# Keys and values of the last pair made inside its recurrence; early routing cut into five pieces

## The reference, cut to what matters

```
x = x + linear_attention_and_ffn(_ln(x), 4 layers)
x = x + cosine_similarity(_ln(x) @ Wv.T, ctx @ Wt.T)
x = x + two_expert_gate(_ln(x))
x = x + state_space_block(_ln(x))
x = x + cross_attention(_ln(x), ctx)
x = x + top2_of_8_experts(_ln(x))

# the state space block, with 512 channels of 16 states each
h[t] = decay[t] * h[t-1] + u[t];  y[t] = sum_n h[t, n] * C[t, n]

# the cross attention, 8 heads of 64
q = x @ Wq;  k = context @ Wk;  v = context @ Wv
out = softmax(q k^T / 8) v;  return out @ Wo + bo

# the routing of 2048 rows to experts that hold 512 rows each
logits = x @ Wr + br;  topv, topi = top_k(logits, 2)
rank = cumsum(one_hot(topi).sum(1)) - ...      # place of the row at its expert
keep = rank < 512
```

## Time and profile before

| | before |
|---|---|
| time, median of 3 runs | 2595.84 us |
| lowest and highest | 2592.74 and 2601.61 us |
| profiled execution, its own time | 2597.52 us |
| its span, first to last instruction | 2595.7 us |
| PE, DVE, ACT, POOL busy, share of the span | 83%, 63%, 40%, 11% |
| granted TensorE clock, mean | 0.90 |
| last recurrence | about 1969 to 2128 us |
| its end, tail and queries | 2128 to 2180 us |
| lone cross attention | 2180 to 2284 us |
| last routing, scatter and the first fetch | 2284 to 2321 us |
| experts | 2321 to 2596 us |

### The profile page before, as it was taken

How to read it: one execution, slowest core, us unless ns; L and a number is a source line. 1 busy time by engine, 2 the same in 40 slices (tenths; PEclk the granted TensorE clock), 3 DMA queues, 4 the chain that set the end, 5 groups by cost and what they waited for, 6 DMA issues and landing times. The chain is left out here.

```text
span 2595.7 us, 31259 instructions
## 1 busy us (share of the span) xinstructions
PE 2153.1 (83%) x11024; PEld 1316.8 (51%) x11024; DVE 1633.6 (63%) x2717; ACT 1029.7 (40%) x1611; POOL 292.2 (11%) x332
## 2 busy tenths in 40 slices
PE   6999999999999988766467887888788778849994
PEld 4666666665666656533123354434354444636662
DVE  6555555555555566545999998989999983220002
ACT  1222222222222222113775876577658752212221
POOL 1111111111111111100000000010000001310005
PEclk8999999999999999877788988988899987759997
DMA  6000100000000000010110111011101102103333
GB/s 221 1 0 17 42 8 0 17 32 17 0 17 25 23 1 0 1 41 18 55 49 23 49 40 51 21 34 39 49 17 55 49 17 73 42 19 102 101 101 113
DMA packets 57469, 102.55 MB, mean 40 GB/s; under 512 B 7828, under 2 KB 39087, under 8 KB 56832
## 3 DMA queue, kind: packets, MB, share of 16 engines
q1 hardware_dynamic: 54272, 93.67, 10.9%
q0 software_dynamic: 3072, 7.28, 0.9%
HBM read 87.10 MB, written 14.94 MB: 39 GB/s over the span
## 5 line engine op out<-in xcount | busy, mean ns | idle before, releaser
L1822 PE MATMUL pa<-arena 128*128 128x512 f32 x512 | 311.3, 739 | 97.7 <-DVE arena L1392 97.6
L1384 DVE TENSOR_TENSOR_SCAN arena<-arena 128x1024 f32<-128x1024 f32 x128 | 292.4, 2284 | 7.9 <-ACT arena L831 7.5
L1608 PE MATMUL po<-arena 128*128 128x256 f32 x1024 | 230.1, 381 | 0.0
L1598 PE MATMUL pa<-arena 128*128 128x512 f32 x512 | 228.0, 598 | 0.8 <-ACT arena L679 0.8
L1822 PEld LDWEIGHTS pa<-arena 128*128 128x128 f32 x512 | 104.5, 223 | 233.8 <-DVE arena L1392 130.4
L694 ACT COPY arena<-po 128x512 f32<-128x512 f32 x64 | 37.5, 586 | 463.1 <-PE po L1563 463.1
L1608 PEld LDWEIGHTS po<-arena 128*128 128x128 f32 x1024 | 191.2, 189 | 31.8 <-issue 3.5
L544 POOL TENSOR_SCALAR arena<-arena 128x2 f32<-128x2 f32 (+1 forms) x92 | 27.6, 300 | 1557.1 <-DVE arena L1251 886.5
L815 ACT ACTIVATE arena<-arena 128x510 f32<-128x510 f32 x256 | 170.4, 716 | 60.1 <-DVE arena L1384 52.8
L1529 PE MATMUL pt<-arena 128*128 128x128 f32 x724 | 113.3, 286 | 74.6 <-DMA arena<-rows_to_experts 19.9
L1081 DVE TENSOR_TENSOR arena<-pa,arena 128x512 f32<-128x512 f32 x256 | 158.4, 681 | 26.1 <-PE pa L1543 25.3
(11 more groups left out here) (264 smaller groups left out, 3736.3 us busy)
## 6 DMA issues: line engine op xcount, KB each, us to landing
arena<-bc_rows SPq DMA_DIRECT2D x64, 512.0 KB, 4.2
arena<-in_L_ffn_W SPq DMA_DIRECT2D x16, 1024.0 KB, 7.5
arena<-in_L_attn_W SPq DMA_DIRECT2D x8, 1024.0 KB, 5.3
rows_to_experts<-arena SPq DMA_DIRECT2D x4, 1024.0 KB, 12.7
arena<-rows_to_experts SPq DMA_DIRECT2D x8, 512.0 KB, 8.6
rows_from_experts<-arena SPq DMA_DIRECT2D x8, 512.0 KB, 3.3
arena<-in_x SPq DMA_DIRECT2D x4, 512.0 KB, 7.2
arena<-in_rows SPq DMA_DIRECT2D x8, 256.0 KB, 3.2
```

The lines of the kernel that those rows point to most:

```text
L1384: v.tensor_tensor_scan(h.rearrange(flat), decay.rearrange(flat), h.rearrange(flat), 0.0, ALU.mult, ALU.add).then_inc(scan_done, 1)
L1598: last = mm(pa[(i + 2) % 4][:, :], w1[:, k, ts(i, P)], yT[:, k, :], start=k == 0, stop=k == KC - 1)
L1608: last = mm(po[s][:, ts(i, D)], gT[:, c, ts(2 * s + i, P)], w2[:, c, :], start=c == 0, stop=c == FM - 1)
L1822: last = mm(pa[c][:, :], ident, uh[i % len(uh)][:, n, :], start=g == 0 and n == 0, stop=g == NS // NG - 1 and n == NG - 1)
```

## The change

Three things are changed.

First, the keys (four steps) and the values (four steps) of the last pair are made by PE in slots 13, 15, 17, 21, 23, 25, 29 and 31 of the last recurrence (`LAST_SLOTS`), each at the end of its slot, all in the one bank `pt[0]`. ACT copies the first seven at the end of the slot behind, the eighth after the last slots of the loop. They are stored in memory whose weights are not used any more (`last_kT`, `last_vv`), since the keys and values of the pair before are still in use. PE waits for the eighth copy before the output product, which writes `pt[0]`. The four key steps in front of the tail are gone, and so are the four value steps at the start of the lone cross attention.

Second, S(0) of the lone cross attention is issued behind the queries, in front of the transposes for the router.

Third, DVE's early routing comes in pieces: `compared`, now only its first three operations, behind M(0); the rest of it, `counted`, behind M(1); `chosen` behind M(2); `ranked` behind M(3); `placed` behind M(4) and the division of tile 0; `weighed` behind M(5). The two counting products on PE go from slot 0 to slot 6. POOL's transfers for tile i wait for W(i+4) instead of W(i).

```diff
+LAST_SLOTS = (13, 15, 17, 21, 23, 25, 29, 31)
@@ POOL, send_rows
-                    pool.wait_ge(av2_done, 16 * (PAIRS - 1) + i + 1)
+                    pool.wait_ge(av2_done, 16 * (PAIRS - 1) + i + 5)
@@ ACT, mixer
+            def last_out(k):
+
+                if k < QC:
+                    late(k, last_kT[:, k, :], bank_head)
+                else:
+                    act.wait_ge(v2_done, TT * p + k - QC + 1)
+                    nc.scalar.copy(last_vv[:, k - QC, :], bank_head[:, :]).then_inc(v2_out, 1)
...
                     if q is not None:
                         cross(i)
+                    if n is None and i - 1 in LAST_SLOTS:
+                        last_out(LAST_SLOTS.index(i - 1))
...
             if p is not None:
-                for k in range(4):
+                if n is None:
+                    last_out(len(LAST_SLOTS) - 1)
+                for k in range(4) if n is not None else ():
                     late(routed + k, kT[:, k, :], late_banks[k])
@@ DVE, early_routing
                 compared(0, NT - TT)
+            if i == 2:
+                counted(0, NT - TT)
+            if i == 4:
                 chosen(0, NT - TT)
-            if i == 1:
+            if i == 6:
                 ranked(0, NT - TT, 1)
+            if i == 8:
                 placed(0, NT - TT)
-            if i == 9:
+            if i == 10:
                 weighed(0, NT - TT, 1)
@@ PE, mixer
+            def last_step(k):
+
+                bank = bank_head[:, :]
+                if k == 0:
+                    pe.wait_ge(w_cross_in, CROSS_W_IN)
+                    pe.wait_ge(ctx_in, 32 * p + 32)
+                elif k <= QC:
+                    pe.wait_ge(late_out, late_base + k)
+                else:
+                    pe.wait_ge(v2_out, TT * p + k - QC)
+                if k < QC:
+                    keys(k, bank)
+                else:
+                    values(k - QC, bank)
...
                 if n is not None:
                     head(i)
+                elif p is not None and i in LAST_SLOTS:
+                    last_step(LAST_SLOTS.index(i))
...
+                else:
+                    pe.wait_ge(v2_out, TT * p + TT)
                 for s in range(2):
...
                     queries(m)
+                if n is None:
+                    pe.wait_ge(late_out, late_base + LATE - 2)
+                    scores2(0, lone_score, last_kT)
             if n is None:
                 rows_routed()
```

More of the change, by code:

```diff
@@ L851, in cross @@
                     last.then_inc(pexp_ready, 1)
-                if i in (0, 2) and at.lone:
-                    for m in range(i, i + 2):
-                        value_out(m, lone_values)
                 if i in VALUE_COPIES and not at.lone:
-                    value_out(VALUE_COPIES.index(i), value_banks)
+                    value_out(VALUE_COPIES.index(i))
                 if i % 2 == 1 and 0 <= (i - 3 - drain) // 2 < 16:
@@ L1155, in compared, with counted @@
             step.after(v.tensor_tensor(tie, tie, mask, ALU.mult))
+        def counted(first, end):
+            up, tie = above[:, first:end], level[:, first:end]
             step.after(v.tensor_tensor(up, up, tie, ALU.add))
@@ L1823, in state_sum, with scores2 @@
                 last.then_inc(ysum_done, 1)
-            def scores2(u):
+            def scores2(u, banks=at.score, keys=last_kT if at.lone else kT):
                 tile, j, e = u // 4, u % 4 // 2, u % 2
@@ L1897, in queries @@
                 last.then_inc(late_done, 1)
+            def last_step(k):
[11 more added lines that the diff above has]
+                    values(k - QC, bank)
             def cross_scores(i):
-                if at.lone and i == 0:
-                    scores2(0)
-                    for m in range(TT):
-                        values(m)
+                if at.lone and i == 6:
                     ranks(0, NT - TT, 1)
```

47 lines of the change are left out of this document (25 added, 22 removed).

## The result

| | before | after |
|---|---|---|
| median of the runs, us | 2604.26 (13 runs) | 2587.0 (13 runs) |
| lowest and highest, us | 2589.48, 2610.44 | 2583.47, 2591.02 |
| ratio after / before, 95% interval | | 0.9949 [0.9933, 0.9966] |
| the profiled execution, us (span) | 2597.52 (2595.7) | 2588.83 (2587.0) |
| granted clock over the span | 0.900 | 0.901 |

The change is 0.51% faster: 13.3 us of 2604, with 8.9 to 17.4 us as the interval. (The ratio takes all runs into account; the two medians alone are 17.3 us apart, since the runs of the kernel before spread over 21 us.) The terms of the forecast add up to 14.2 us less (21.2 - 7.0). Its 2582 us starts from a median of three runs, 2595.84; over 13 runs that median is 2604.26. So the gain is the better comparison: 0.54% was forecast.

A forecast was written before the change was run, and what follows sets the result against it. DVE was taken to bound the last recurrence, PE the window beginning with the keys. From 2597.52 us, minus 21.2 plus 7.0 gave 2583.3; less 1.7 for a median, 2582 us, 0.54% faster, range 2572 to 2594.

The forecast's parts named there:

- Bias to W(0): Start of the lone cross attention: chain M(0), three `compared` operations, M(1), E(1), C(0) takes 6.3 us, 11.2 us less.
- the values alone: Start of the lone cross attention: values on PE are hidden beside the routing, so taking only them away gives nothing.
- W(0) to W(4): Lone cross attention: counting products add 1.2 us, `placed` instead of `weighed` saves 0.4, so 0.8 us more.
- The tail: Behind the recurrence: without the keys, transposes start 11.9 us earlier; S(0) costs 1.1, so the router's bias comes 10.8 us earlier.
- the late output product: End of the recurrence: steps in slots 29 and 31 cost about 2.0 us together, 0.8 given back for clock, 1.2 net.
- The recurrence: Last recurrence: ACT waiting for steps before copying makes scans late; costs 4.8 + 1.0 + 1.2 = 7.0 us.
- the late E in front of L1365: Last recurrence: late E before each L1365 holds up the product with Wo, 0.5 us twice, 1.0 us.
- W(4) to the end of the lone cross attention: Rest of the lone cross attention: order as before, so no change in time, 0 us.
- Full clock in the lone cross attention: Rival, lone cross attention: half clock doesn't come, turns about 3.7 us instead of 4.76, 6 us less, 2576; chance 0.18.
- The copies were not free: Rival, last recurrence: copies fit ACT's 1.81 us gap and its lead, recurrence costs 1 to 2 us, 2577; chance 0.12.
- None of the eight steps ran at half clock: Rival, last recurrence: five of seven steps meet the half clock, 11 us more, 2593; chance 0.14.
- that last rival: Slower, last recurrence: PE becomes the bound, 8 us lost per pair of units, 2598 to 2600 and more; chance 0.06.

The follow-up runs named there:

- the pieces alone: Only the early routing cut into pieces, with counting products in slot 6 and POOL's new pacing, against the kernel before: 2597.5 us, ratio 0.9991.
- the late copies: Changed kernel, but ACT copies each step two slots behind it instead of one: 2578.27 us, ratio 0.9921 to the kernel before.
- the doubled steps: Changed kernel with the first six steps done twice: 2597.09 us, ratio 0.9981; the same with copies one slot later: 2584.67 us, ratio 0.9945.
- the kernel with two a turn: Kernel with copies one slot later plus two unread 384-column matmuls per even slot from 12 on in the lone cross attention: 2571.69 us, ratio 0.9896.
- the wait in the tail filled: Five unread 512-column matmuls before the tail's transposes, added to the kernel with two unread 384-column matmuls per even slot: 2567.28 us, ratio 0.9886.

## Why the prediction was right, and where its steps were not

**Bias to W(0) (-11.5, predicted -11.2).** Right, and by the chain given: M(0), three operations of `compared`, M(1), E(1), C(0). That the values alone would give nothing was nearly right (1.7 us). What the prediction didn't say is that the pieces alone would give only 5.3. Its term for this stage was right; that the gain would last to the end was not shown by it, and is the subject of the last item below.

**W(0) to W(4) (+0.4, predicted +0.8).** Right. The turn with the counting products has 5.55 us instead of 4.76, and the division's turn 7.47 instead of 7.90.

**The tail (-11.7, predicted -9.6 with the late output product).** The wait taken away is 12.0 us by the rows, not 11.9. The start of the product was right: 1.85 us later, predicted 2.0. The clock was undersold. That product gave back 1.6 us in its first half, where I had allowed 0.8, and the queries another 1.2, where I had none: they began at half clock and did not stay there.

**The recurrence (+10.6, predicted +5.8 up to scan 31).** The mechanism was right, as the late copies and the doubled steps show, and the late scans nearly so: for a group of three 0.1, 1.6 and 0.8 us were predicted, for the units 15, 17 and 19; measured were 1.12, 0.40 and 0.80 for 17, 19 and 20, then 1.11, 0.79 and 1.52 for 25, 27 and 28, 5.7 for 4.8 in all. The waits at the units 20 and 28 were not foretold. The term that was too small is the one for the late E in front of L1365, "I take 0.5 us twice": the two waits grew from 0.74 to 2.10 and 3.69, 4.3 us more in place of 1.0. I had the E late by what its own copy costs. In the trace C(8), the tile's copy and the decays behind it all come first on ACT, so the delays add up; the second of the two also met T and the product with Wo at half clock (3.07 us for 1.90).

**W(4) to the end of the lone cross attention (+8.8, predicted 0).** "The order is as before" was true and not enough. The prediction took the clock of this stretch as unchanged, and no row said that it would be. In the ten profiles without added matmuls there, the stretch takes 64 to 74 us with nearly the same work, and its clock goes up and down: in the kernel after it is 0.65, 0.78 and 0.50 in the three windows of 4 us from 2212 on. The runs say that not all of this loss is there in every pair of runs: the four stages that the change was meant for sum up to -12.2 us, and the runs gave -13.3 [-17.4, -8.9]. With the full +8.8 it would be -3.4, which the interval excludes. The profile of before lay 6.7 us under the median of these runs, so its 64.27 us may be the better of its cases; the kernel before has one profile here, so how often it takes which case stays open, and so does what share of the +8.8 the new places of the pieces cause.

**The rivals.** Full clock in the lone cross attention did not come (0.50 in the window behind the bias). The prediction tied the fall to the wait for C(0), which shrank from 4.60 us to 0.86; the clock fell all the same, and earlier, at the end of the router's matmuls: 1.00 in the window up to 2173.8 and 0.50 from 2174 on, 6 us ahead of W(0). The copies were not free. None of the eight steps ran at half clock, each took 2.1 us; some of the T beside them and one product with Wo did. PE did not become the bound: it is busy 118.90 of 155 us. Two things in that last rival are wrong as written. Its 2598 to 2600 us are the price of three lost pairs of units; four would give about 2607. And it was not state sums that brought the clock back each time: behind scan 13 of the recurrence before, two of the five times it came back within a product with Wo.

So the forecast came true in its sum, 14.2 us for 13.3, and that is in part luck. Two terms were off by +4.8 and -2.1 us, a third was missing, and the 13.3 us of the runs hold something that this pair of profiles does not show, since its stages add up to 3.7.

## What to carry to other kernels

A copy out of PSUM on an engine that works in order costs its wait and not only its duration: put it where the matmul it waits for is surely done. One slot later gave 10.0 and 11.1 us in the recurrence here, and a ratio of 0.9921 against 0.9949, for a change of two lines. Two things that hide each other (values on PE, routing on DVE) must be taken away together, and each alone tells little. A gain at the start of a stage is to be followed to its end: here the clock behind it took most of it back in the profile. Where the clock of a chain of narrow matmuls rises and falls again, add one unread matmul a turn and look at the granted clock: it was worth 0.57% here (0.9864 against 0.9921), more than the change itself.

## What the runs showed of the hardware

PE being busy does not by itself bring the full clock. In the kernel after, W, T and S followed each other from 2179.89 to 2199.8 us without a gap at 0.50. It came back 3.6 to 15.7 us behind W(4), with unread matmuls and without. With them (one or two of 384 columns a turn, or twelve of 64) it then stayed at 1.00 for 44 to 58 us, without them for 14 at most. What brings it back stays open.

The clock also fell without a long idle time of PE: with the wait in the tail filled, PE had waited at most 0.82 us at a time in the 12 us before 2160, and the clock went from 1.00 to 0.50 as the router's matmuls of 8 columns ran.

Twelve matmuls of 128x64 took 2.89 us at full clock, 0.24 each, and two of 128x384 1.56 (in the kernel with two a turn), so a column costs 3.8 ns in the narrow ones and 2.0 in the wide ones.
